# Seven products in the second group of three sequences, norms of the first rows in two parts, and a transpose queued behind P

## The reference, cut to what matters

```
x = x + layernorm(attention(layernorm(x)))
x = x + layernorm(ffn(layernorm(x)))

attention(x): q = relu(x Wq + bq); k = relu(x Wk + bk); v = relu(x Wv + bv)
    e = q k^T / sqrt(512), causal;  p = softmax(e);  y = p v
    return relu(y Wo + bo)
ffn(x): two gated score branches (softmax, top 32 of 512) around x @ weight, plus bias
```

## Time and profile before

| | us |
|---|---|
| median of 3 runs | 2065.27 (2065.19 to 2065.55) |
| profiled execution, own time | 2064.47 |
| its span, first to last instruction | 2062.7 |

### The profile page before, as it was taken

One profiled execution on the slowest core, in us unless ns is written; L12 is line 12 of the kernel. 1 busy time (PEld: TensorE's weight loads), 2 busy tenths in 40 slices (PEclk: granted clock), 3 DMA queues, 4 the chain that ended last, 5 costly groups with the idle time before them and its releaser, 6 DMA issues. The chain is left out here.

```text
span 2062.7 us, 35450 instructions
## 1 busy us (share of the span) xinstructions
PE 1989.9 (96%) x11327; PEld 1127.2 (55%) x11327; DVE 1626.7 (79%) x3372; ACT 1159.4 (56%) x2568; POOL 1210.7 (59%) x1365
## 2 busy tenths in 40 slices
PE   7999999999999999999999999998999999999997
PEld 3766655666565666665556666454444444444443
DVE  7686766687676677776667766678999999999998
ACT  5545433455443445544335444335888888888885
POOL 3446352344534345535235462325999999999997
PEclk9999999999999999999999999999999999999998
DMA  7667665455766546665646475451222223223221
GB/s 236 159 176 150 173 172 133 124 143 154 181 160 152 134 128 169 140 178 133 163 111 169 142 162 130 110 159 49 82 98 88 88 88 105 95 88 98 88 78 67
DMA packets 350702, 270.64 MB, mean 131 GB/s; under 512 B 241970, under 2 KB 273842, under 8 KB 350516
## 3 DMA queue, kind: packets, MB, share of 16 engines
q1 hardware_dynamic: 331796, 205.71, 37.9%
q10 hardware_dynamic: 18720, 62.66, 10.6%
HBM read 145.34 MB, written 65.01 MB: 102 GB/s over the span
## 5 line engine op out<-in xcount | busy, mean ns | idle before, releaser
L824 PE MATMUL psum<-v,pT 128*128 128x512 f16 x1632 | 365.5, 381 | 10.7 <-DMA pT<-rows 10.6
L824 PE MATMUL psum<-kT,qT 128*128 128x512 f16 (+3 forms) x1920 | 363.6, 347 | 0.1
L824 PEld LDWEIGHTS psum<-kT,qT 128*128 128x128 f16 x1920 | 180.9, 98 | 176.1 <-DVE rows L1657 1.3
L824 PEld LDWEIGHTS psum<-v,pT 128*128 128x128 f16 x1632 | 160.1, 98 | 193.9 <-issue 15.7
L850 PE MATMUL psum<-hT_early,ring 128*128 128x256 f16 x2304 | 259.4, 273 | 0.0
L2008 DVE MAX8 c<-cut 128x8 f32<-128x512 f32 x384 | 244.5, 678 | 0.0
L850 PEld LDWEIGHTS psum<-hT_early,ring 128*128 128x128 f16 x2304 | 225.5, 98 | 33.7
L824 PE MATMUL psum<-fw,xsT 128*128 128x512 f16 x768 | 178.8, 383 | 0.7 <-ACT xsT L1450 0.7
L824 PE MATMUL psum<-w_o,vT 128*128 128x512 f16 x768 | 173.7, 382 | 4.4 <-ACT kT L1183 3.4
L824 PE MATMUL psum<-fw,h2T 128*128 128x512 f16 x768 | 176.2, 379 | 0.0
L2004 DVE MATCH_REPLACE8 cut<-c,cut 128x512 f32<-128x512 f32 x256 | 170.9, 675 | 0.0
(11 more groups left out here) (205 smaller groups left out, 4174.8 us busy)
## 6 DMA issues: line engine op xcount, KB each, us to landing
ring<-wc_scratch ACTq DMA_DIRECT2D x109, 512.0 KB, 4.6
xg<-x SPq DMA_DIRECT2D x64, 256.0 KB, 5.6
xr<-x SPq DMA_DIRECT2D x64, 256.0 KB, 3.3
h_scratch<-hb SPq DMA_DIRECT2D x64, 256.0 KB, 3.0
h<-h_scratch SPq DMA_DIRECT2D x64, 256.0 KB, 2.7
x<-x_scratch SPq DMA_DIRECT2D x64, 256.0 KB, 3.0
x_scratch<-xr SPq DMA_DIRECT2D x62, 256.0 KB, 2.4
out<-zn SPq DMA_DIRECT2D x59, 256.0 KB, 2.0
```

The source lines that it names most:

```text
L824: mm = nc.tensor.matmul(outp, stat(a), mov(c), start=(n == 0 and k == 0), stop=(n == total - 1 and k == 2))
```

## The change

It has four parts.

1. `opening` is now true for the first-tile groups and for group 2 alone. Groups 6, 10 and 14 take the seven products. What belongs to that moves too: seven split parts and four differences for their rows, made in groups 5, 9 and 13; three more transposes each; and two more weight pieces for each of their projections.
2. In a first-tile group, `transpose_h` of parts 0 and 2 moves from step 4 to step 5, behind the transpose of P.
3. In group 0, the norms of tiles 2 and 3 of group 1 move from step 2 to step 3 on DVE, behind the low halves of q.
4. The split of the mixed v weights moves from step 4 to 5, and their store from step 5 to 6. It signals `w_in[4]` instead of `wc_out`, so that the waits on `wc_out` are for the plain weights alone; the load of the first residual tile (which has the same memory) waits for it, and ACT's wait before k of group 2 counts it in.

```diff
 def opening(g):
-    return 0 < g <= NG and GROUP * (g - 1) % TILES in (0, GROUP)
+    return first_tiles(g) or g == 2
...
-                                .then_inc(wc_out if kind == "v" else w_in[4], 16)
+                                .then_inc(w_in[4], 16)
...
                 def load_residual(T):
+                    if T == 0:
+                        sp.wait_ge(w_in[4], 16 + 32 * 4)
...
-                    if h == 4 and g + 1 < NG:
+                    if h == (5 if first_tiles(g) else 4) and g + 1 < NG:
                         transpose_h(g + 1, 0, 2)
...
-                    if H in (5, 10):
-                        store_mixed(VQK[H // 5 - 1])
+                    if H in (6, 10):
+                        store_mixed("v" if H == 6 else "q")
...
                     if (kind, g, o) == ("k", 2, 0):
-                        act.wait_ge(w_in[4], 16 + 32 * 8)
+                        act.wait_ge(w_in[4], 16 + 32 * 4 * len(VQK))
...
                     if (kind, g, n) == ("v", 1, 0):
-                        act.wait_ge(wc_out, 32 * 4 * (len(VQK) + 1))
+                        act.wait_ge(wc_out, 32 * 4 * len(VQK))
...
-                    if H in (4, 8, 10):
-                        mixed_hi({4: "v", 8: "q", 10: "k"}[H])
+                    if H in (5, 8, 10):
+                        mixed_hi({5: "v", 8: "q", 10: "k"}[H])
...
                         if g == 0:
-                            dve.wait_ge(wc_out, 32 * 4 * (len(VQK) + 1))
+                            dve.wait_ge(wc_out, 32 * 4 * len(VQK))
...
-                    if H in (4, 9, 11):
-                        mixed_lo({4: "v", 9: "q", 11: "k"}[H])
+                    if H in (5, 9, 11):
+                        mixed_lo({5: "v", 9: "q", 11: "k"}[H])
...
                         if h == 2:
-                            for j in range(GROUP):
+                            for j in range(GROUP if g else 2):
                                 ln_norm(g + 1, j)
+                        if H == 3:
+                            for j in range(2, GROUP):
+                                ln_norm(1, j)
```

## The result

The changed kernel takes 2067.22 us (median of 20 runs, 2064.72 to 2074.11) against 2063.36 of the kernel before in the same session (20 runs, 2058.07 to 2066.93). The ratio is 1.0021, 95% interval 1.0013 to 1.0029: slower by 0.2%, some 4.3 us. The forecast was 2060.9 us, 4.4 us under the median of 2065.27 us known then. The time lies within the range given, but on the other side of no change, where the prediction had put 19%.

What follows compares the result with a forecast made beforehand. PE was taken to bound the kernel nearly everywhere. From 2064.47 us, the opening's -4.0 and the pairs' -0.4 gave 2060.1 in the profiled execution's time; the median, 0.8 above, was forecast at 2060.9 us, range 2049 to 2070.

Steps and rivals of the forecast that it cites:

- The sum for a pair: Groups 5 and 6 walked through: 140.4 us; against now, the three pairs change by -0.9, +0.9 and -0.4 us.
- at nothing on PE: Groups 5, 9, 13: the added POOL instructions, high parts, transposes and weights cost PE nothing; row statistics wait about 2 us.
- split 1.4 us later than now: Second groups of the pairs: P of the fourth tile is split 1.4 us later, if the group starts where it does now.
- 11.8 were to be had: Ceiling of part 1 on PE: 1.31 us saved per projection, 3 projections in 3 groups, only where PE sets the pace.
- The walk of DVE and ACT: Group 6 in program order: waits for ACT's copies lose 3.4 of 3.9 us at k's product 3, some 2 before product 5.
- Rival D: Groups 6, 10, 14: P of the first tile, behind transposes of parts 4 to 6, comes late; 10.5 us, 2071.4; chance 0.12.
- over 143 us: Sign: pairs of groups over 143 us, with a wait for P in step 1, would show that Rival D holds.
- Rival E: POOL's added work holds back DVE, 0.7 us for each of seven instructions, 5 us a pair: 2075.9; chance 0.06.
- Part 2: Group 5: P goes out first, behind three weight pieces, lands 6.1 to 6.9 us after issue; wait 2.6 to 3.9, not 3.92.
- The bound by DVE's k half: Step 7 scores need k's last low half from DVE: at most 2.8 us (group 5) and 0.8 (group 9) can be won.
- The opening: Parts 3 and 4: one wait of 2.6 us left, output products 2.7 us earlier; -4.1 us in all, taken as -4.0.
- under the ones that slowed PE: Opening: a 2.6 us wait is too short to slow the 24 matmuls behind it, so 1.44 us are gained too.

Runs made afterwards that it cites:

- e8_no_seven: Changed kernel without part 1 (groups 6, 10 and 14 keep four outputs): 2056.05 us, ratio 0.9965 to the kernel before.
- e4_fourth_p: Changed kernel, with P of the fourth tile transposed ahead of parts 0 and 2 in groups 6, 10 and 14 too: 2062.42 us, ratio 1.0000 to the kernel before.
- e6_norms: e4_fourth_p, with the norms of tiles 2 and 3 moved from step 2 to step 3 in groups 6, 10 and 14: 2060.55 us.
- e7_weights_v: e4_fourth_p, with v's first two weight pieces sent one step later in groups 6, 10 and 14: 2062.11 us.
- f2_no_late: Changed kernel, with 32-byte-a-partition DMAs instead of the three transposes of parts 4 to 6 for groups 6, 10 and 14: 2069.49 us.
- e10_all: Changed kernel with the edits of e4_fourth_p, e5_weights_k, e6_norms and e9, and v's second weight piece moved to the start of step 1: 2067.6 us.
- e3: Changed kernel, with P of the first tile transposed ahead of parts 4 to 6 at the end of groups 5, 9 and 13: 2078.84 us.
- e5_weights_k: e4_fourth_p, with k's two added weight pieces sent one step later, behind P, in groups 1, 5, 9 and 13: 2063.31 us.
- f1_no_pieces: Changed kernel, with 32-byte-a-partition DMAs instead of the weight pieces added for groups 6, 10 and 14: 2067.93 us.
- e1_opening: Kernel before, with parts 3 and 4 of the change alone: 2060.62 us, ratio 0.9981.
- e2_seven: Kernel before, with part 1 of the change alone: 2078.66 us, ratio 1.0077.
- e9: e8_no_seven, with k's two last low halves written earlier on DVE in step 5 of groups 1, 5, 9 and 13: 2051.31 us.

## Why the prediction was wrong

**What failed.** Part 1 was put at no gain and no loss, and costs 11.6 us. The sum for a pair had one price in it, the copies and sums in the second group, and two others were at nothing. The first failed step costs what moves into groups 5, 9 and 13, and the new weights and transposes, "at nothing on PE". It named all of them: seven instructions of POOL, three transposes, 768 KB beside 512. But it asked only when each was wanted, not what it keeps from P. P1 costs 5.8 us. The second is P of the fourth tile in groups 6, 10 and 14: "split 1.4 us later than now", and no wait was priced for it. It costs 6.6 us. By the table, against e8_no_seven, these two come with 6.3 us of copies and 0.7 in the first-tile groups, which is less than the scatter. PE's matmuls are 4.3 us shorter (1983.2 against 1987.5 busy) where 11.8 were to be had. Of the 7.5 us missing some 6.1 are matmuls at the lower clock behind waits, and 1.7 of these stand in the opening and are not part 1's. The waits less what PE saves make 6.6 + 5.8 + 6.3 + 0.7 - 4.3 = 15.1, near the difference of the two profiled spans (2069.9 - 2054.3 = 15.6); the timed difference is smaller, so the shares hold for the profiled executions. That the time still fell into the range is due to the range's width, which reached 2070, 9 us above the forecast.

**"P of the fourth tile is split 1.4 us later."** It was the place that cost most. Counted from the group's start, P's low halves end at 49.2 us in all three groups before, and at 52.8, 51.7 and 53.3 in groups 6, 10 and 14 of the changed kernel: 2.6 to 4.1 us later. Parts 0 and 2 of the next rows are later by more, 6.1 to 7.7 us, and so leave SP right ahead of P instead of well before it. In group 14 they ended at 1195.2 and P came at 1195.7; before they ended at 1188.9 and P at 1192.9. What holds them is not a difference of POOL (the one of this step starts at 1193.8, behind their issue) but the residual row, whose wait for ACT stands ahead of the low parts on POOL. POOL and SP before, then in the changed kernel:

```profile
1183.84 1.27 POOL L2168 TENSOR_TENSOR xr<-ob,xr 128x512 f32<-128x512 f32 x1 [1.59 <-ACT ob L1279]
1186.30 2.60 SPq L626 DMA_TRANSPOSE hT_early<-hhl  x2
...
1190.16 1.27 POOL L2173 TENSOR_TENSOR xr<-ob,xr 128x512 f32<-128x512 f32 x1 [5.50 <-ACT ob L1281]
1192.62 2.59 SPq L626 DMA_TRANSPOSE hT_early<-hhl  x2
```

ACT's `ob` stands there behind high quarters of q, which wait for q's sums on DVE: the work that part 1 adds to the second groups themselves. This is read from the trace. e4_fourth_p shows by experiment that the order behind those two transposes is what makes PE wait.

**The walk of DVE and ACT.** Right in place, too dear in size. It had 3.4 us at k's product 3 and 2 at product 5, in part the same loss, so nearly all of the 11.8 us to be won in three groups. The copies take 6.3 us: 0.3 in group 6, which has its wait for P ahead of them, and 2.8 and 3.2 in groups 10 and 14. PE waits 1.6 us at k's product 3 there and at most 0.4 at a product 5, but also 1.2 us at k's first product, for the bank of q's second sum, which the walk had not looked at. In e6_norms, with two norms moved, these waits halve.

**Rival D.** Right in mechanism for group 6, where P1 costs 3.19 us and 1.6 of slow matmuls. The low parts 4 to 6 ended 5.7 us into the group (3.9 forecast), P was issued at 466.4, 7.3 us in (8 forecast), and landed in up to 9.0 (6.9 forecast). But its reason was only half right. The three transposes do not slow P's landing by themselves; v's megabyte, into which P now falls, does (e7_weights_v, f2_no_late). The pairs were over 143 us once, not three times. Rival E was given 0.06. The contention is shown by e10_all, at 2 us in one place, not at 5 in a pair; in the changed kernel the differences add 0.2 us at that place.

**Part 2.** P was ready at 438.5 and issued at 438.6 (both are 3.2 us earlier than before by the opening alone), so the queue's 0.9 us were won as forecast. It landed in 5.1 us in group 5 and PE waited 2.50. The forecast was 2.6 to 3.9, though its own landing of 6.1 gives 441.5 + 6.1 = 447.6 and so 3.1 at the least. The 2.50 is a lucky execution: with the same code up to there PE waited 3.68 to 5.01 (e3, e4, e6, e7, f2), about as long as the 3.92 before. The wait was there for k's two added pieces: without them the landing in group 5 is 2.8 to 2.9 (e5_weights_k, f1_no_pieces). The bound by DVE's k half was sound: it is the wait that e8_no_seven has left. There the first pair is 2.6 us shorter than in e1_opening (2.8 given) and the second not at all (0.8 given, with 1.7 of slow matmuls); the third, not priced, is 3.2 shorter.

**The opening.** The norms and the later split did what was worked out: one wait of 2.47 us (2.6 forecast). Group 1 starts 3.2 us earlier, of 4.1 forecast. The step that failed in it: a wait "under the ones that slowed PE" was to leave the matmuls fast. In the changed kernel's profiled execution the 24 took 7.04 us. In others they took 5.35 behind the same wait, so that the 1.44 us were gained in some executions and not in others (see the last section).

## What to carry to other kernels

When a change lowers the matmuls of an engine that is the bound, list the transfers and helper instructions that it adds, and ask for each burst which small urgent transfer lies in it; a deadline of one's own is not the only cost. Where several waits stand within 2 us of each other, taking one away shows the next: f1_no_pieces and e5_weights_k removed 5.7 and 7.5 us of waits for P of the fourth tile and gained nothing. Take apart a change of several parts before it is judged: here parts 2 to 4 are worth 7 us and part 1 loses 11.6. And profile a kernel more than once before a wait of 2 us is explained: here the same code gave 2.50 and 5.01.

## What the runs showed of the hardware

**The issue of a transpose can block its queue.** The issue of one chunk of P takes 1.24 us on SP in the usual case. It took 4.10 us in e2_seven and 6.42 us in the changed kernel's group 14, and what is behind it on SP waits too. It also took up to 4.5 us in group 14 of the kernel before. In these cases two to four weight pieces had been issued on ACT in the 5 us around it. But that is not enough: in group 5 of the changed kernel three pieces went out from 436.1 on, the issue at 438.6 took 1.24 us, and only the landing was long (5.1). What decides between the two was not tested.

**A small transfer lands late in a burst.** P of the first tile takes 2.3 to 2.8 us to land in e7_weights_v and 5.0 to 9.0 in the changed kernel, for v's megabyte beside it. In the ten us from 470 of e5_weights_k, where PE idles for 4.09 us on P, the DMA engines moved 288 GB/s, where they moved 154 to 171 over the first pair of the kernels before and after; the granted clock (ahead of the DMA share) is 0.83:

```profile
470.00:480.00 10.00, 5.91 (x27) 2.77 (x26) 6.84 (x12) 2.81 (x6) 5.19 (x6) 0.83 1.10 288
```

**The length of a wait does not tell by itself whether the clock falls.** Twelve matmuls of P times v take 2.75 us at 2.4 GHz. Behind 2.50 us of idle they took 4.44 (changed kernel, group 5), behind 3.90 they took 5.28 (e3_first_p, group 5), but behind 3.31 only 2.75 (e3_first_p, group 9), and behind 1.81 also 2.75 (changed kernel, group 13). The opening shows that the kernel does not decide it either. Twelve profiled executions have the same code there and the same wait of 2.46 to 2.47 us. In eight the 24 matmuls behind it took 7.03 to 7.04 us, and in four (e3, e8, e9, e10) 5.35 to 5.36. The changed kernel from 48 to 52 us, then e8_no_seven:

```profile
48.00:50.00 2.00, 2.00 (x8) 0.78 (x7) 0.90 (x2) 1.65 (x2) 0.28 (x1) 0.68 0.39 87
50.00:52.00 2.00, 2.00 (x6) 0.70 (x5) 1.45 (x1) 0.48 (x1) 2.00 (x1) 0.50 0.00 0
...
48.00:50.00 2.00, 2.00 (x11) 0.88 (x9) 0.89 (x2) 1.90 (x2) 0.02 (x1) 1.00 0.55 123
50.00:52.00 2.00, 2.00 (x11) 0.91 (x10) 1.71 (x1) 0.26 (x1) 2.00 (x1) 1.00 0.00 0
```

The granted clock is 0.68 and 0.50 in the one, so at the lower level of 1.2 GHz in the second stretch, and 1.00, which is 2.4 GHz, in the other. That is 1.7 us of a kernel's time which no edit here made. What makes the difference stays open.
